# State-space recurrence on one core: a quarter of the products B*dt*u taken to ScalarE in the turned layout

## What is computed

```python
u = silu(conv(x @ W_in.T)); x_dbl = u @ W_x.T
dt = softplus(x_dbl[..., :4] @ W_dt.T + b_dt)
Bs, Cs = x_dbl[..., 4:20], x_dbl[..., 20:36]
def step(h, inp):                      # one time step
    dA = exp(dt_t[..., None] * A)      # 128 channels x 16 states
    h = dA * h + (dt_t * u_t)[..., None] * B_t[:, None, :]
    return h, einsum('bdn,bn->bd', h, C_t)
y = ys + u * D_skip;  out = (y * silu(z)) @ W_out.T
```

## Time and profile before

| | us |
|---|---|
| Median of 3 runs | 763.95 |
| Lowest and highest run | 763.78, 768.19 |
| Span of the profiled execution, first to last instruction | 766.2 |
| Recurrence in it, first product to the end of the last scan | 47.0 to 472.3 |
| Attention and feed-forward after it | about 476 to 766 |

### The profile page before, as it was taken

The page is one execution under the profiler, slowest core; times in us unless marked ns, Lnnn a source line. Parts: engine busy times, 40 slices in busy tenths (PEclk is TensorE's granted clock), DMA queues, the critical chain, the costliest instruction groups (busy, mean ns, idle before and its releaser), DMA issues.

```text
span 766.2 us, 10774 instructions
## 1 busy us (share of the span) xinstructions
PE 607.6 (79%) x3563; PEld 257.1 (34%) x3591; DVE 570.3 (74%) x587; ACT 440.7 (58%) x662; POOL 474.0 (62%) x252
## 2 busy tenths in 40 slices
PE   3876686777986777967868879978976969999993
PEld 2321121121221212311212223446663335777741
DVE  3488998998998999999989997445562525666643
ACT  1887767587578677676775752544444224555520
POOL 6369999999999999999999998500002200000002
PEclk9999798898998998997989999989999889999997
DMA  3389677576665676666765761000000000000002
GB/s 96 83 266 297 220 240 234 199 260 232 215 237 216 223 255 216 241 229 204 261 231 201 255 228 58 1 1 2 2 12 3 6 15 1 2 1 2 1 2 60
DMA packets 33187, 105.47 MB, mean 138 GB/s; under 512 B 6997, under 2 KB 7518, under 8 KB 33118
## 3 DMA queue, kind: packets, MB, share of 16 engines
q1 hardware_dynamic: 32022, 103.94, 40.1%
q10 hardware_dynamic: 776, 0.55, 0.3%
q0 software_dynamic: 320, 0.13, 0.1%
HBM read 98.84 MB, written 2.10 MB: 132 GB/s over the span
## 4 chain that ended last, share of the span: by engine, by line
issue 34%; PE 24%; POOL 16%; DVE 15%; ACT 7%; DMA 2%; POOLq 0%; SPq 0%; DVEq 0%; ACTq 0%
POOL dbu L1733 7%; POOL hc L1722 7%; DVE hh_all L1434 7%; PE py L702 6%; DVE pb L1429 3%; PE py L229 2%; PE pb L198 2%; PE pb L690 2%; PE px L252 1%; PE px L729 1%; DMA cc<-scr 1%; POOL yg L1736 1%; DVE yg L1443 1%; ACT pb L1155 1%; DVE dtu_all L1415 1%
## 5 line engine op out<-in xcount | busy, mean ns | idle before, releaser
L1722 POOL TENSOR_TENSOR hc<-hh_all,cc 128x1024 f32<-128x1024 f32 x128 | 299.2, 2367 | 2.8 <-DMA cc<-scr 1.5
L702 PE MATMUL py<-hc,w_cst 64*64 64x512 f32 x1024 | 157.0, 673 | 26.3 <-POOL hc L1722 17.9
L1736 POOL TENSOR_TENSOR yg<-w_xs 128x512 f32<-128x512 f32 x12 | 15.2, 1266 | 247.2 <-DVE w_xs L1560 154.6
L1434 DVE TENSOR_TENSOR_SCAN hh_all<-da,pb 128x1024 f32<-128x1024 f32 x72 | 164.6, 2287 | 2.5
L1434 DVE TENSOR_TENSOR_SCAN hh_all<-pb,dbu 128x1024 f32<-128x1024 f32 x56 | 127.7, 2281 | 17.8 <-POOL dbu L1733 14.4
L1733 POOL TENSOR_TENSOR dbu<-bb,dtu_all 128x1024 f32<-128x1024 f32 x56 | 132.6, 2369 | 0.0
L690 PE MATMUL pb<-bc,w_sel 128*128 128x512 bf16 x118 | 42.2, 424 | 71.3 <-DVE hh_all L1434 67.3
L1155 ACT ACTIVATE pb<-dt_all,w_aneg 128x1024 f32<-128x1024 f32 x56 | 62.6, 1118 | 59.9 <-DVE hh_all L1434 58.2
L1429 DVE TENSOR_TENSOR pb<-pb,dtu_all 128x1024 f32<-128x1024 f32 x72 | 87.5, 1215 | 1.8 <-DVE dtu_all L1415 0.2
L285 DVE TENSOR_REDUCE gate_all<-pb 128x1 f32<-128x1024 f32 (+7 forms) x64 | 60.4, 986 | 32.8 <-PE pb L208 16.8
L1155 ACT ACTIVATE da<-dt_all,w_aneg 128x1024 f32<-128x1024 f32 x72 | 80.5, 1137 | 0.5
(11 more groups left out here) (290 smaller groups left out, 952.6 us busy)
## 6 DMA issues: line engine op xcount, KB each, us to landing
cc<-scr SPq DMA_DIRECT2D x128, 512.0 KB, 4.4
bb<-scr SPq DMA_DIRECT2D x56, 512.0 KB, 4.8
w_xs<-hc SPq DMA_DIRECT2D x6, 256.0 KB, 4.6
w_xst<-in_x SPq DMA_DIRECT2D x2, 512.0 KB, 5.3
scr<-bcf SPq DMA_DIRECT2D x8, 128.0 KB, 3.6
w_xs<-dt_all SPq DMA_DIRECT2D x4, 256.0 KB, 6.0
w_xs<-dtu_all SPq DMA_DIRECT2D x4, 256.0 KB, 5.6
out<-yg SPq DMA_DIRECT2D x8, 128.0 KB, 2.7
```

The costliest lines, as they stand in the source:

```text
L702: last = nc.tensor.matmul(py[part(t), half(r)], ident[part(r), part(r)], hc[u % NHC][part(r), half(t)], start=(n == 0), stop=(n == NS - 1) ...
L1434: nc.vector.tensor_tensor_scan(hh[u % NHH][:, :], decay[:, :], drive[:, :], 0.0, ALU.mult, ALU.add).then_inc(scan_done, 1)
L1722: nc.gpsimd.tensor_tensor(hc[u % NHC][:, :], hh[u % NHH][:, :], cc[u % NCC][:, :], ALU.mult).then_inc(hc_done, 1)
```

## The change

GpSimd makes the drive of 5 states instead of 7 (`POOLED` = (1, 5, 8, 11, 13)), VectorE that of 7 instead of 9, and 4 states (`CROSSED` = (3, 6, 10, 15)) get theirs in a new way. At the start of a sequence TensorE turns `dtu` (8 transposes of 128 x 128 through `px`) and ScalarE copies it to `dtu_t`, in which a partition is a time step of a block of 128; then TensorE turns B (8 transposes of 32 x 128) and ScalarE copies it to `b_t`. In this layout B_n is one number per partition and block, so the product is a scaled copy: 8 activations of 128 x 128 per unit into `cross`. TensorE turns them back with 8 transposes into `pb[u % 2]`, from where the scan reads its drive. There is one `cross` buffer.

The pieces of the preparation move one state later, since `px` is now used at n = 0 (`pe_x` to n = 1, `act_x` to n = 2, and so on; `pe_out_late` to n = 15, `act_out` stays). `AHEAD` = 2 puts the double exponential there. `pe_x` and the last gate wait for the copies out of `px`. Three semaphores of the prologue and of the hand-over to the last stage are merged with others.

```diff
-        POOLED = (1, 4, 6, 8, 10, 12, 14)
+        POOLED, CROSSED = (1, 5, 8, 11, 13), (3, 6, 10, 15)
-        LAST, UNITS, SKIP_AT, AHEAD = NSEQ - 1, NS * NSEQ, 8, 1
+        LAST, UNITS, SKIP_AT, AHEAD = NSEQ - 1, NS * NSEQ, 8, 2
+        def pe_dtu_t(pe, q):
+            for h in range(2):
+                pe.wait_ge(px_free[h], freed(q + 1))
+                for j in range(4):
+                    last = nc.tensor.transpose(px[h][:, block_at(j)], dtu[q % 2][:, block_at(4 * h + j)], ident)
+                last.then_inc(dtu_turned, 1)
+            pe.wait_ge(dtu_t_done, 2 * q + 1)
+            for j in range(8):
+                last = nc.tensor.transpose(px[0][:, 32 * j:32 * j + 32], bcf[:, block_at(j)], cst[0:32, IDN:IDN + 32])
+            last.then_inc(b_turned, 1)
+        def pe_cross(pe, u):
+            atleast(pe, scan_done, u - 1)
+            for j in range(8):
+                if j % 4 == 0:
+                    pe.wait_ge(cross_done, 2 * cross_count(u) + j // 4 + 1)
+                last = nc.tensor.transpose(pb[u % 2][:, block_at(j)], cross[:, block_at(j)], ident)
+            last.then_inc(cross_full, 1)
         def pe_b(pe, u):
+            if crossed(u):
+                pe_cross(pe, u)
+                return
@@ block.tensor
                 pe_sum(pe, u - LAG)
+                if n == 0:
+                    pe_dtu_t(pe, q)
-                        if n == 0:
+                        if n == 1:
                             pe_x(pe, q + 1, h)
-                        if n == 10 + h:
+                        if n == 11 + h:
                             pe_dt_add(pe, q + 1, h)
-                    if n == 1:
+                    if n == (2 if q < LAST else 1):
                         pe_gate(pe, q, h)
-                        if n == 14 and h == 0:
+                        if n == 15 and h == 0:
                             pe_out_late(pe, q // 2 - 1)
+        def act_dtu_t(act, q):
+            for h in range(2):
+                act.wait_ge(dtu_turned, 2 * q + h + 1)
+                nc.scalar.activation(dtu_t[:, half(h)], px[h][:, :], ACT.Copy).then_inc(dtu_t_done, 1)
+            act.wait_ge(b_turned, q + 1)
+            nc.scalar.activation(b_t[:, :, :], px[0][:, 0:256].rearrange("p (j n) -> p j n", n=32)[:, :, 0:NS], ACT.Copy).then_inc(b_t_done, 1)
+        def act_cross(act, u, t):
...
+            for j in range(4 * t, 4 * t + 4):
+                last = nc.scalar.activation(cross[:, block_at(j)], dtu_t[:, block_at(j)], ACT.Copy, scale=b_t[:, j, n:n + 1])
+            last.then_inc(cross_done, 1)
+            CROSS_AT = [[(v, t) for v in CROSSED for t in range(2) if n == (v - 3 + t if v > 12 else v - 2)] for n in range(NS)]
@@ block.scalar
+                if n == 0:
+                    act_dtu_t(act, q)
...
+                for v, t in CROSS_AT[n]:
+                    act_cross(act, u - n + v, t)
@@ dve_unit
+                if crossed(u):
+                    dve.wait_ge(cross_full, cross_count(u) + 1)
+                else:
                     k = own_count(u)
...
```

More of the change, by code:

```diff
@@ L437, in pool_count, with crossed, cross_count, da_count @@
             return NP * (u // NS) + sum(1 for n in POOLED if n < u % NS)
+        def crossed(u):
+            return u % NS in CROSSED
+        def cross_count(u):
+            return len(CROSSED) * (u // NS) + sum(1 for n in CROSSED if n < u % NS)
+        def da_count(u):
+            return u - pool_count(u)
         def own_count(u):
-            return u - pool_count(u)
+            return da_count(u) - cross_count(u)
+        def block_at(j):
+            return slice(128 * j, 128 * j + 128)
         def outs_before(q):
@@ L1149, in act_exp @@
             else:
-                k = own_count(u)
+                k = da_count(u)
                 if k >= NDA:
-                    behind = next(v for v in range(u - NDA, -1, -1) if not pooled(v) and own_count(v) == k - NDA)
+                    behind = next(v for v in range(u - NDA, -1, -1) if not pooled(v) and da_count(v) == k - NDA)
                     act.wait_ge(scan_done, behind + 1)
@@ L1426, in dve_unit @@
             else:
[L1427 to L1431 removed]
+                if crossed(u):
+                    dve.wait_ge(cross_full, cross_count(u) + 1)
+                else:
+                    k = own_count(u)
+                    dve.wait_ge(b_full, k + 1)
+                    nc.vector.tensor_tensor(pb[u % 2][:, :], pb[u % 2][:, :], dtu[q % 2][:, :], ALU.mult).then_inc(dbu_done, 1)
+                    dve.wait_ge(dbu_done, k + 1)
+                decay, drive = da[da_count(u) % NDA], pb[u % 2]
             dve.wait_ge(da_done, u + 1)
```

71 lines of the change are left out of this document (41 added, 30 removed).

## The result

The changed kernel takes 788.34 us, the median of four runs (785.55 to 789.69), against 764.16 for the kernel before on the same chip. The ratio is 1.0305, with a 95% interval of 1.028 to 1.0331. It is slower by 3%, and outside the forecast range of 733 to 770. The profiled execution spans 785.7 us, where before it was 766.2.

What follows compares the result with a forecast made beforehand. GpSimd was taken to bound the kernel at 53.25 us per sequence. Sequence 0 -3.2, six sequences -14.1 (50.9 each), boundaries +7.85, sequence 7 -2.8 sum to -12.2: 763.95 to 751.8, said as 752 us, range 733 to 770.

Steps and rivals of the forecast that it cites:

- The engines' sums: Predicted work per sequence after the change: GpSimd 48.7 us, VectorE 47.8, ScalarE 47.1, TensorE 46.2.
- the two figures that the prediction set side by side: ScalarE's 32 scaled copies of 128 columns per sequence: 8.6 us from the trace, 9.3 by the skill page.
- Step 1: TensorE, sequence start: projection and turning back unit 3 precede the last sum, so the gate comes 1.4 us late.
- the walk: The prediction's step-by-step timing of one sequence, t = 0 at VectorE's first product; it gave 50.9 us per sequence.
- Step 2: GpSimd after the late gate: drive 11 ready at 33.7, wanted at 33.6; the late sum is one stall of 1.5 us.
- Step 3: ScalarE's way to dt begins with exp(11) after scan 9, VectorE has one product less meanwhile: dt 1.3 us late.
- Step 4: Three image boundaries: later output projection and `act_out` delay scan 1 and the gate; 7.85 us in all.
- GpSimd as the bound: Rival: GpSimd stays the bound and the waits hide; at most -37.1 us, 727, or 735 with a third; chance 20%.
- The saving is eaten: Rival: each of 32 crossed units costs one more wait of about 0.4 us, 12.8 us in all: 764; chance 18%.
- Slower: Rival: ScalarE becomes the bound at 0.37 us per copy, deciding from 0.34, with 5 us of waits: 780; chance 12%.

Runs made afterwards that it cites:

- e_dense: Changed kernel with preparation back at its old states, turns at n = 13, 5 pooled, units 4 and 9 crossed, 9 own: 789.63 us, ratio 1.0321.
- e_wide: Changed kernel with eight scaled copies of 128 columns per crossed unit replaced by two of 512 (product not the reference's): 770.99 us, ratio 1.0065.
- e_three: Changed kernel with only units 3, 10 and 15 crossed, unit 6 VectorE's own again: 779.07 us, ratio 1.0169.
- e_shift: Changed kernel with no crossed units, turns or their copies; 7 pooled (3 instead of 4), 9 own, preparation still one state later: 788.26 us, ratio 1.0312.
- e_bound3: Changed kernel, preparation at old states, crossed 0, 4, 15; sequences 3 and 5: sum and spread between projection halves, gate projection one state later: 796.95 us, ratio 1.0415.
- e_six: Kernel before with state 14 given from GpSimd to VectorE (6 pooled, 10 own), nothing else: 765.35 us, ratio 1.0024.

## Why the prediction was wrong

**The engines' sums were right.** Per sequence of 57.06 us (from the gate at 110.44 to that at 452.82, over six) the engines' work follows from the busy times of the changed kernel between 100 and 440 us (PE, PEld, DVE, ACT, POOL, clock, DMA):

```profile
100.00:440.00 340.00, 273.39 (x1460) 97.38 (x1458) 287.40 (x175) 282.51 (x478) 292.85 (x127) 0.92 0.59 197
```

VectorE is busy 287.40 / 340 x 57.06 = 48.2 us per sequence (forecast 47.8), ScalarE 47.4 (47.1), TensorE 45.9 (46.2), GpSimd 49.1 (48.7). All four were met within 0.4. Eight 128-column copies and the next instruction start 288.23 - 285.90 = 2.33 us apart, 0.29 for each, where 0.27 was taken. So 32 cost 9.3, the larger of the two figures that the prediction set side by side. The rows that it put beside it read PSUM and could not tell the price from SBUF.

The fault is in what was added to 47.8. Sequence 4, from 268.91 to 324.17, is 55.3 us, and by its waits on VectorE it closes: 48.2 busy, 3.3 at the gate (forecast 1.5), 2.8 for dt in two pieces (1.3), 1.0 small ones (0.3).

**Step 1, the late gate: the place right, the size half.** The start of sequence 4 in the changed kernel, TensorE:

```profile
273.03 1.75 PE L748 MATMUL py<-hc,w_cst 64*64 64x512 f32 x8
274.71 2.07 PE L650 MATMUL px<-w_xs,w_wts 128*128 128x512 f32 x2
278.38 1.02 PE L651 MATMUL px<-w_xs,w_wts 128*128 128x512 f32 x2
279.24 1.03 PE L722 MATMUL pb<-w_cst,cross 128*128 128x128 f32 x8
280.20 1.09 PE L748 MATMUL py<-hc,w_cst 64*64 64x512 f32 x8
```

The order is that of the walk. The last sum ends at 281.3, 12.4 after the first product at 268.91, where the walk had 10.5. The sum of unit 14 takes 1.7 and the projection 274.71 to 279.24 = 4.5, against 0.9 and 3.5 in the walk. Those came from the earlier trace rows. Here TensorE did them in part at half clock, behind short waits for a copy and for scan 0: 1.75 us for this sum against 1.09 for the eight matmuls of the last one. That is the mis-sized term. Sequence 1 of the changed kernel shows it without any edit, for there the granted clock stayed at 1.00. The instructions and waits are the same, the sum takes 1.0, the projection 3.5, and the gate waits 1.6, as forecast. In sequences 2, 4 and 6, with the clock fallen, it waits 3.2 to 3.3. TensorE in sequence 1, VectorE's gate there, and the granted clock (the last but two) in sequence 1 and in 4:

```profile
103.79 1.09 PE L748 MATMUL py<-hc,w_cst 64*64 64x512 f32 x8
104.81 1.13 PE L650 MATMUL px<-w_xs,w_wts 128*128 128x512 f32 x2
...
108.35 1.03 PE L722 MATMUL pb<-w_cst,cross 128*128 128x128 f32 x8
```
```profile
110.44 1.29 DVE L1519 TENSOR_TENSOR yg<-py,gate_all 128x512 f32<-128x512 f32 x2 [1.62 <-PE py L748]
```
```profile
103.00:109.00 6.00, 5.75 (x24) 2.54 (x25) 5.79 (x4) 5.98 (x12) 6.00 (x3) 1.00 0.60 236
273.00:276.00 3.00, 3.00 (x11) 0.98 (x11) 2.96 (x3) 3.00 (x9) 3.00 (x2) 0.55 0.51 184
```

Back in sequence 4, GpSimd's product 2 started at 281.5, right behind.

**Step 2** held as far as it went: GpSimd's drives are no longer waited for (0.8 us).

**Step 3, dt: the step that failed.** It let the way to dt start "held until scan 9 has ended", and sized the wait by lengths from there. ScalarE in the changed kernel, sequence 4, then VectorE at dt:

```profile
303.41 1.10 ACT L1203 ACTIVATE pb<-dt_all,w_aneg 128x1024 f32<-128x1024 f32 x1
...
308.17 1.28 ACT L1171 ACT_TABLE_LOAD   x1
309.46 1.07 ACT L1171 ACTIVATE px<-px 128x512 f32<-128x512 f32 x2
310.55 1.28 ACT L1203 ACT_TABLE_LOAD   x1
311.84 1.12 ACT L1203 ACTIVATE pb<-dt_all,w_aneg 128x1024 f32<-128x1024 f32 x1
313.18 0.60 ACT L1179 ACTIVATE dt_all<-px 128x512 f32<-128x512 f32 x1 [0.22 <-PE px L685]
```
```profile
299.54 4.46 DVE L1510 TENSOR_TENSOR_SCAN hh_all<-da,pb 128x1024 f32<-128x1024 f32 x2
313.81 0.69 DVE L1488 TENSOR_TENSOR dtu_all<-px,u_all 128x512 f32<-128x512 f32 x1 [2.55 <-ACT dt_all L1179]
```

Scan 9, the first of the two in that row, had ended at about 301.8. exp(11) waited for nothing and began at 303.41, for ScalarE was still at work: 1.6 late. Its way from there to the copy of dt took 9.8 us, shorter than the 10.5 of the earlier trace rows, and without the 1.6 the wait would be 2.55 - 1.6 = 0.95, below the forecast. The lateness was built up earlier. From exp(5) at 284.84 to dt at 313.18 ScalarE has 28.3 us of work with hardly a gap, 4.7 of it copies; VectorE, from the end of scan 3 at 284.7 to 311.2, where it stands ready for `dve_dtu`, has 26.5 less 0.2 of waiting, 26.3. The average over a sequence, 47.1 beside 48.7, could not show that. e_dense, e_wide and e_three show it from three sides. But the copies make only part of the wait: with fewer of them or cheaper ones, 12.1 and 11.9 us are left between 100 and 440, and without any 12.8 (e_shift), 2.0 to 2.1 a sequence. That part fits the step's own reason, one product less ahead of `dve_dtu`, which it had put at 1.5 and cut to 1.3 in case TensorE were faster; it wasn't, its granted clock was 0.50 from 312 to 314 us. The other 7 us or so, of 19.7, are the lateness of ScalarE that the step had no term for. Sequence 0, which has no gate, waits 3.0 for dt by itself.

**Step 4, the boundaries: right in kind, half in size.** Sequences 3 and 5 take 6.0 us more than the mean of the four others, 54.7, where 2.9 was forecast. At the start of sequence 5 in the changed kernel, ScalarE, then VectorE:

```profile
327.29 1.30 ACT L1227 ACTIVATE w_xm<-px 64x512 f32<-64x512 f32 x2 [6.76 <-PE px L775]
328.71 1.12 ACT L1203 ACTIVATE pb<-dt_all,w_aneg 128x1024 f32<-128x1024 f32 x1
```
```profile
329.92 2.29 DVE L1510 TENSOR_TENSOR_SCAN hh_all<-pb,dbu 128x1024 f32<-128x1024 f32 x1 [2.22 <-ACT pb L1203]
339.90 1.29 DVE L1519 TENSOR_TENSOR yg<-py,gate_all 128x512 f32<-128x512 f32 x2 [4.24 <-PE py L748]
352.69 1.23 DVE L1505 TENSOR_TENSOR pb<-pb,dtu_all 128x1024 f32<-128x1024 f32 x1 [1.50 <-PE pb L736]
374.58 0.69 DVE L1488 TENSOR_TENSOR dtu_all<-px,u_all 128x512 f32<-128x512 f32 x1 [3.28 <-ACT dt_all L1179]
```

Scan 1 waits 2.2 behind `act_out` (1.6 forecast) and the gate 1.0 more than in sequence 4, which together is what the step meant: 3.2. Beside sequence 4, sequence 5 is 5.5 longer; the rest came later, 1.5 at unit 7's spread and 1.0 at dt, less 0.5 of small waits. The walk took a late start to be paid once. Here it was paid again where an engine had no gap to catch up.

**The rivals.** GpSimd as the bound fell at once, by the 47.6 us for which it waited for TensorE. "The saving is eaten" was nearest in mechanism: it let waits eat the gain, though in small pieces at each crossed unit. They stood at the gate and at dt, few and large, and took the forecast gain of 12.2 us on the span and 19.5 more. "Slower" put its price on the copy and said it decides from 0.34. Its 780 was nearest in time. The copy cost 0.29, and the kernel is slower still: the price alone wasn't the point, the place was. All cases let a shift of the preparation by one state be nearly free except at the boundaries, and e_shift shows that, with work as before, this shift and one other pooled state (3 for 4) make 23 us.

What stays open: how much of e_shift's 23 us its pooled set makes, which has state 3 where before it had 4, since no run changed the one without the other; why the same code behind the last scan takes 286.0 us in one kernel and 296.9 in another; and the 30.3 us at the end of e_bound3.

## What to carry to other kernels

When a change levels the engines' sums, the largest sum may stop being a forecast, as it did here: in a loop where four in-order engines release each other, compare ScalarE's work with VectorE's between each two waits, not over the period. A piece of work moved out of a gap need not be free even by one step: ask what gap it filled, at what clock it will run after the gap, and what stands behind it in its queue. Try the levelling first in the cheapest way that the kernel has (here e_six, one state moved), since that tells whether the time follows the sums at all. And compare the edited stage by itself, not only the whole time.
